# Two groups of heads share one burst of value sums, one copy, one turn and one normalisation in a two-layer gated cross-attention kernel

## The chip, the core and the metric

One core of a Trainium2 chip. The metric is the device time of one execution in microseconds (us). The engines are TensorE (PE, with its weight loads as PEld), VectorE (DVE), ScalarE (ACT), GpSimd (POOL) and SyncE (SP), which issues nearly all DMAs.

## What is computed

32 images of 256 tokens with 256 channels pass through two layers. The change lies in the first one, attention over the 120 context rows and the 256 tokens of the image itself, 16 heads of 16 channels:

```python
def _L0_xattn_ref(x, context, w_qkv, w_proj, b_proj):      # x here is layernorm(x)
    qkv = (x @ w_qkv.T).reshape(B, N, 3, H, D).transpose(2, 0, 3, 1, 4)
    q, k, v = (qkv[0], qkv[1], qkv[2])
    kv = context.reshape(B, N_c, 2, H, D).transpose(2, 0, 3, 1, 4)
    k = jnp.concatenate([kv[0], k], axis=2)
    v = jnp.concatenate([kv[1], v], axis=2)
    attn = jax.nn.softmax(jnp.einsum('bhnd,bhmd->bhnm', q * scale, k), axis=-1)
    out = jnp.einsum('bhnm,bhmd->bhnd', attn, v)
    return out.transpose(0, 2, 1, 3).reshape(B, N, C) @ w_proj.T + b_proj
x = x + tanh(g_xattn[0]) * _L0_xattn_ref(layernorm(x), ctx_2048, ...)
```

A ternary linear layer, a gated recurrence with a linear layer and an int8 linear layer follow. They run in a second phase of the kernel ("rows") that the change doesn't touch.

## The kernel before

**Phases.** All images stay in SBUF (`xs`). The attention phase (`*_attention`) goes over the images in `iterations`, from -3 to 32, since an image is prepared up to three iterations ahead and finished in the one after its own. Then the rows phase does the other three layers.

**An iteration** has 24 slots (`HS`, variable `u`). In slot u TensorE makes the transposed scores of two heads for one tile of 128 keys: two matmuls into one of three banks `st_ps` (L682, `scores_t`). ScalarE turns them into probabilities by one exp of 128x512 (L1022) into a ring of 12 tiles (`PR`), `probs`. A slot's scores need the exp of three slots before. Three k-tiles times two pairs, six slots, make up one group of four heads (`HG`), and there are four groups (`NG`).

**Maxima.** The exps need the row maxima of the scores, which go into the transposed product as three more rows of the queries. So TensorE also makes each head's scores the other way round (`scores`, L692, 376 keys wide, two banks `ms_ps`), 32 of them in an iteration, one or two a slot (`maxima_of`), mostly for the next image. VectorE reduces each to negated maxima (L932). POOL splits the maxima into three bf16 parts (`split_neg`, L535 to L541), TensorE turns them (jobs `neg0` and `neg1`, L748, weights of 24 columns), ScalarE copies them (`neg_rows`, L1029), and SP moves them by DMA into the queries' rows (L449, L466). neg1 is for the second half of the image's slots (12 on), neg0 for the first half of the next image.

**Value sums.** When a group's six slots are through, `attend` multiplies its three k-tiles with the values: per k-tile four heads side by side, each a product with weights of 32 columns (16 values, a one for the sum of the probabilities, and zeros) into 32 partitions of `pv_ps`. The matmuls are f32 and stand as two each in the trace, 24 for the 12 of a group (L707). The bursts stand in slots 7, 13, 19 and, for the last group, in slot 1 of the next iteration. ScalarE copies `pv_ps` to `oT` (`copy_o`, L1035, slots 8, 14, 20 and 2), TensorE turns it in two transposes (jobs `o0` to `o3`, L754, slots 10, 16, 22 and 4) into the bank `aux`, and VectorE takes the reciprocal of the sums (L939) and multiplies (L941, `normalise`), which frees the bank. At last `aT` (L759) turns the four groups' `attn`, ScalarE copies it, and `proj` multiplies with the output weights (L738); VectorE adds the result to `xs` (`update`, L974).

**What sets the order.** Two tables written out by hand. `JOBS` gives every TensorE job its bank (0 is `misc`, 1 is `aux`), its first slot, its number of slots and the image that it is for. A job waits until the job before it in its bank is taken, whoever takes it: q, k, v and xT by ScalarE, proj by VectorE's update; in `aux` kcT, neg and aT by ScalarE, o by VectorE. `AT` gives ScalarE's and VectorE's small steps their slots: ScalarE does a slot's small steps and then its exp, VectorE a slot's first maximum, the small steps and the slot's further maxima. All five engines run their queues in order. In a slot TensorE does the transposed scores, one row of maxima scores, the jobs in the table's order, a burst if there is one, and the rest of the maxima's scores.

**Queries and keys.** Jobs xT (L722), q and k (L730) and v (L733) make them from the normalised image; ScalarE copies q (L1070), k (L1090) and the context's keys `kc` (L1059) into `qk`. POOL splits `qk` into three bf16 parts (L552 to L558), half by half, with `split_neg` for neg0 between the halves. SP's ten DMAs a half (`stack`, L432 to L437) bring the parts into place, and SP issues the DMA of neg0 (L466) between the two halves.

Of the kernel before, what the change touches and what calls it, by code (L numbers as in the profile page):

```python
# [15 lines left out]
def flamingo_two_layers(  # L16
# [38 lines left out]
    NG = H // HG  # L55
    HS = NG * NKT * 2
# [28 lines left out]
    with ExitStack() as ctx:  # L85
# [51 lines left out]
        oT = sb("oT", [P, S])  # L137
        rcp = sb("rcp", [P, T, 4])
# [184 lines left out]
        def live(b):  # L323
# [9 lines left out]
        }  # L333
        AT = {
            "cxp": 0, "xnT": 1, "copy_o": 2, "kc": 4, "csq": 5, "q": 6, "aT": 5, "neg1": 7, "xn": 13, "k": 11, "decay": 17,
            "vcx": 14, "neg0": 19, "v": 23,
            "stats0": 0, "aggr0": 5, "norm": 4, "update": 19, "stats1": 20, "aggr1": 23, "mx": 6, "mn": 7,
# [287 lines left out]
        def tensor_attention(pe):  # L625
# [44 lines left out]
            def body(i, par):  # L670
# [24 lines left out]
                def attend(B, pB, w):  # L695
# [3 lines left out]
                    if k == 0:  # L699
                        wait(pe, s_oT, B * NG + g)  # L700
# [5 lines left out]
                    for j in range(HG):  # L706
                        mm = pe.matmul(pv_ps[VW * j:VW * (j + 1), 0:S], v[0:rows, pB, k, HG * g + j, :],  # L707
                                       probs[0:rows, (2 * w + j // 2) % PR, j % 2 * S:(j % 2 + 1) * S],
                                       start=(k == 0), stop=(k == NKT - 1), skip_group_check=True)
                    mm.then_inc(s_pv, 1)  # L710

                def make(name, part, off):
# [37 lines left out]
                    elif name[0] == "o":  # L750
                        g = int(name[1])
                        pe.wait_ge(s_oT, (b + off) * NG + g + 1)
                        for t in range(T):
                            mm = pe.transpose(aux[:, t * P:(t + 1) * P], oT[:, t * P:(t + 1) * P], ident[:, :])  # L754
                    elif name == "aT":
                        wait_taken(pe, b, "o3")
# [14 lines left out]
                for u in range(HS):  # L771
# [30 lines left out]
        def vector_attention(dve):  # L802
# [121 lines left out]
            def body(i, par):  # L924
# [539 lines left out]
```

## Time and profile before

| | us |
|---|---|
| Median of three runs | 1093.32 (1092.88 to 1097.19) |
| The profiled execution | 1093.88, its span 1092.1 |
| TensorE busy | 1029.8 (94%) |
| VectorE busy | 875.0 (80%) |
| ScalarE busy | 794.0 (73%) |
| GpSimd busy | 699.0 (64%) |

The attention phase takes the first 900 us of the span and the rows phase the rest. TensorE's granted clock is full in the attention phase. A busy time is the union of an engine's instructions; the ends of matmuls are modelled, and matmuls overlap each other in the array, so for TensorE the distance from one start to the next tells more than the durations. In a timeline like instructions in a row are merged into one line, with the first one's start and their count.

### The profile page before, as it was taken

What the parts mean: (1) busy time and instruction counts of PE and PEld (TensorE: products, weight loads), DVE (VectorE), ACT (ScalarE), POOL (GpSimd) and SP (SyncE); (2) the same over time, 40 slices, a digit from 0 to 9 for tenths busy, and PEclk for the clock granted to TensorE, in tenths of its full rate; (3) what the DMA queues carried; (4) which work ended last, traced back from release to release, by engine and by line L of the source; (5) the groups of instructions that cost most, each with busy time, mean ns of one, the idle gap of its engine ahead of it and who ended that gap; (6) DMA issues with size and microseconds to landing.
All of it is one profiled execution on the core that took longest, in us unless ns stands there. A gap on an engine that the chain in (4) does not pass through costs nothing. (4 is left out here: it accounts for less than half of the span.)

```text
span 1092.1 us, 26149 instructions
## 1 busy us (share of the span) xinstructions
PE 1029.8 (94%) x8522; PEld 706.0 (65%) x8522; DVE 875.0 (80%) x2218; ACT 794.0 (73%) x1731; POOL 699.0 (64%) x1348
## 2 busy tenths in 40 slices
PE   4799999999999999999999999999999967999994
PEld 3356666666666666666666666666666545888873
DVE  6767888878888878888887888888778765999996
ACT  3367777777777777777777777777777647999983
POOL 6556666666666666666666666666665214677776
PEclk8799999999999999999999999999999987999997
DMA  7775555655555556555556555555555210233232
GB/s 147 102 114 110 116 108 107 106 105 106 113 114 108 106 106 110 111 111 108 115 113 111 109 109 108 109 112 111 100 101 92 57 33 25 69 105 102 96 112 78
DMA packets 140906, 111.29 MB, mean 102 GB/s; under 512 B 15650, under 2 KB 136932, under 8 KB 140772
## 3 DMA queue, kind: packets, MB, share of 16 engines
q1 hardware_dynamic: 140068, 109.07, 49.6%
q8 instruction: 69, 1.13, 0.5%
q10 hardware_dynamic: 704, 0.55, 0.3%
q14 instruction: 65, 0.53, 0.2%
HBM read 30.33 MB, written 16.32 MB: 43 GB/s over the span
## 5 line engine op out<-in xcount | busy, mean ns | idle before, releaser
L932 DVE TENSOR_REDUCE neg<-ms_ps 128x1 f32<-128x376 f32 x1024 | 526.5, 544 | 160.1 <-PE ms_ps L692 154.3
L1022 ACT ACTIVATE probs<-st_ps 128x512 f32<-128x512 f32 x768 | 442.5, 603 | 25.2 <-PE st_ps L682 24.6
L692 PE MATMUL ms_ps<-qk 96*128 96x376 bf16 x1024 | 334.4, 327 | 11.6 <-DMA qk<-parts 5.7
L682 PE MATMUL st_ps<-qk 99*128 99x256 bf16 x1536 | 294.9, 274 | 0.7 <-DMA qk<-negT 0.7
L682 PEld LDWEIGHTS st_ps<-qk 99*128 99x128 bf16 x1536 | 133.7, 98 | 125.8 <-issue 41.4
L707 PE MATMUL pv_ps<-probs,v 128*32 128x256 f32 (+1 forms) x3072 | 194.4, 383 | 0.0
L730 PE MATMUL misc<-xnT,wqkvT 128*128 128x256 f32 x512 | 154.9, 386 | 1.7 <-DVE wqkvT L814 0.9
L692 PEld LDWEIGHTS ms_ps<-qk 96*128 96x128 bf16 x1024 | 98.8, 97 | 76.6 <-DVE neg L932 49.6
L707 PEld LDWEIGHTS pv_ps<-probs,v 128*32 128x32 f32 (+1 forms) x3072 | 96.1, 110 | 55.8 <-ACT probs L1022 12.3
L552 POOL TENSOR_SCALAR parts<-qk 128x632 bf16<-128x632 f32 x63 | 45.7, 725 | 125.1 <-ACT qk L1090 125.1
L730 PEld LDWEIGHTS misc<-xnT,wqkvT 128*128 128x128 f32 x512 | 92.1, 194 | 6.5 <-ACT qk L1070 1.8
L1029 ACT COPY negT<-aux 24x256 bf16<-24x256 bf16 x64 | 22.9, 357 | 97.3 <-PE aux L748 97.3
L558 POOL TENSOR_TENSOR parts<-qk,parts 128x632 bf16<-128x632 f32 x63 | 88.1, 1398 | 5.2
L554 POOL TENSOR_TENSOR qk<-qk,parts 128x632 f32<-128x632 f32 x63 | 87.8, 1394 | 5.2
L535 POOL TENSOR_SCALAR negp<-neg 128x16 bf16<-128x16 f32 x64 | 13.1, 205 | 103.2 <-DVE neg L932 103.2
L738 PE MATMUL misc<-wprojT,attnT 128*128 128x256 f32 x256 | 77.3, 385 | 0.8 <-ACT attnT L1073 0.8
L1244 PE MATMUL st_ps<-winT,probs 128*128 128x256 f32 x256 | 70.0, 396 | 8.2 <-ACT probs L1378 8.1
L733 PE MATMUL misc<-wqkvT,xnT 128*128 128x256 f32 x256 | 77.2, 382 | 0.0
L1244 PEld LDWEIGHTS st_ps<-winT,probs 128*128 128x128 f32 x256 | 46.3, 191 | 19.2 <-ACT probs L1378 13.8
L1035 ACT COPY oT<-pv_ps 128x256 f32<-128x256 f32 x128 | 47.5, 371 | 4.4 <-PE pv_ps L707 4.2
L754 PE MATMUL aux<-ident,oT 128*128 128x128 f32 x256 | 48.8, 272 | 0.6 <-ACT oT L1035 0.6
L1090 ACT COPY qk<-misc 128x512 f32<-128x512 f32 x32 | 18.8, 587 | 41.9 <-PE misc L730 41.9
(201 smaller groups left out, 1757.0 us busy)
## 6 DMA issues: line engine op xcount, KB each, us to landing
qk<-parts SPq DMA_DIRECT2D x253, 94.0 KB, 3.6
qk<-parts SPq DMA_DIRECT2D x128, 158.0 KB, 3.6
qk<-parts SPq DMA_DIRECT2D x256, 64.0 KB, 3.5
out_dram<-xn SPq DMA_DIRECT2D x32, 256.0 KB, 2.2
xs<-in_x SPq DMA_DIRECT2D x31, 256.0 KB, 2.9
cx<-in_ctx SPq DMA_DIRECT2D x32, 240.0 KB, 4.0
recurrence_input<-u_in SPq DMA_DIRECT2D x32, 120.0 KB, 2.8
plug<-plugs SPq DMA_DIRECT2D x32, 120.0 KB, 3.4
```

Source lines behind the costliest of these rows:

```text
L554: pool.tensor_tensor(f, f, parts[:, m, 0, :], ALU.subtract).then_inc(s_split, 1)
L558: pool.tensor_tensor(parts[:, m, 2, :], f, parts[:, m, 1, :], ALU.subtract).then_inc(s_split, 1)
L682: mm = pe.matmul(st_ps[u % SR][:, j * S:(j + 1) * S], k6[0:KM, r, h, k * P:(k + 1) * P], q6[0:KM, r, h, :], start=True, stop=True)
L692: pe.matmul(ms_ps[t][:, 0:KEYS], q6[0:KR, r, h % HU, t * P:(t + 1) * P], k6[0:KR, r, h % HU, 0:KEYS], start=True, stop=True).then_inc(s_ms, 1)
L707: mm = pe.matmul(pv_ps[VW * j:VW * (j + 1), 0:S], v[0:rows, pB, k, HG * g + j, :], probs[0:rows, (2 * w + j // 2) % PR, j % 2 * S:(j % 2 + ...
L730: mm = pe.matmul(misc[:, x0 * S:(x0 + 1) * S], wqkvT[:, x1, at:at + P], xnT[:, par, x1, :], start=(x1 == 0), stop=(x1 == KT - 1), skip_gro ...
L733: mm = pe.matmul(misc[:, x0 * C:(x0 + 1) * C], xnT[:, opp, x1, x0 * P:(x0 + 1) * P], wqkvT[:, x1, 2 * C:3 * C], start=(x1 == 0), stop=(x1 ...
L738: mm = pe.matmul(misc[:, x0 * C:(x0 + 1) * C], attnT[:, x1, x0 * P:(x0 + 1) * P], wprojT[:, x1, :], start=(x1 == 0), stop=(x1 == KT - 1), ...
L754: mm = pe.transpose(aux[:, t * P:(t + 1) * P], oT[:, t * P:(t + 1) * P], ident[:, :])
L932: dve.tensor_reduce(neg[:, m, t, h % HU:h % HU + 1], ms_ps[t][:, 0:KEYS], AX.X, ALU.max, negate=True).then_inc(s_red, 1)
L1022: act.activation(probs[:, u % PR, :], st_ps[u % SR][:, :], ACT.Exp).then_inc(s_exp, 1)
L1244: pe.matmul(m1_ps[q][:, t * C:(t + 1) * C], yxT[:, k, t * P:(t + 1) * P], winT[:, k, :], start=(k == 0), stop=False)
```

## The change

`pv_ps` has 512 columns, of which 256 were used. Now groups 0 and 1 go into its two halves in one burst of six k-tiles in slot 13, and groups 2 and 3 in one in slot 1 of the next iteration. One copy of 128x512, four transposes, one reciprocal and one multiplication take the place of two each. The jobs o0 to o3 become o0 and o1. In both tables other steps get new slots: the maxima's turns neg1 (slot 7 to 6) and neg0 (20 to 19), kcT (2 to 3), and on ScalarE and VectorE cxp, xnT, copy_o, q, aT, xn, k, decay, vcx, neg0, aggr0, update, stats1, mx and mn.

```diff
+    NH = NG // 2
-        oT = sb("oT", [P, S])
-        rcp = sb("rcp", [P, T, 4])
+        oT = sb("oT", [P, 2, S])
+        rcp = sb("rcp", [P, T, 2 * HG])
         JOBS = {
             "xT": (0, 1, 1, 2), "q": (0, 3, 4, 2), "k": (0, 8, 4, 2), "proj": (0, 15, 4, -1), "v": (0, 20, 4, 1),
-            "kcT": (1, 2, 1, 2), "o3": (1, 4, 1, -1), "aT": (1, 5, 1, -1), "neg1": (1, 7, 1, 0), "o0": (1, 10, 1, 0),
-            "o1": (1, 16, 1, 0), "neg0": (1, 20, 1, 1), "o2": (1, 22, 1, 0),
+            "kcT": (1, 3, 1, 2), "o1": (1, 4, 1, -1), "aT": (1, 5, 1, -1), "neg1": (1, 6, 1, 0), "o0": (1, 16, 1, 0),
+            "neg0": (1, 19, 1, 1),
         }
         AT = {
-            "cxp": 0, "xnT": 1, "copy_o": 2, "kc": 4, "csq": 5, "q": 6, "aT": 5, "neg1": 7, "xn": 13, "k": 11, "decay": 17,
-            "vcx": 14, "neg0": 19, "v": 23,
-            "stats0": 0, "aggr0": 5, "norm": 4, "update": 19, "stats1": 20, "aggr1": 23, "mx": 6, "mn": 7,
+            "cxp": 1, "xnT": 0, "copy_o": 4, "kc": 4, "csq": 5, "q": 7, "aT": 6, "neg1": 7, "xn": 12, "k": 12, "decay": 21,
+            "vcx": 11, "neg0": 20, "v": 23,
+            "stats0": 0, "aggr0": 0, "norm": 4, "update": 18, "stats1": 23, "aggr1": 23, "mx": 1, "mn": 6,
         }
...
-                    if k == 0:
-                        wait(pe, s_oT, B * NG + g)
+                    if k == 0 and g % 2 == 0:
+                        wait(pe, s_oT, B * NH + g // 2)
-                        mm = pe.matmul(pv_ps[VW * j:VW * (j + 1), 0:S], v[0:rows, pB, k, HG * g + j, :],
+                        mm = pe.matmul(pv_ps[VW * j:VW * (j + 1), g % 2 * S:(g % 2 + 1) * S], v[0:rows, pB, k, HG * g + j, :],
...
-                        g = int(name[1])
-                        pe.wait_ge(s_oT, (b + off) * NG + g + 1)
+                        half_ = int(name[1])
+                        pe.wait_ge(s_oT, (b + off) * NH + half_ + 1)
                         for t in range(T):
-                            mm = pe.transpose(aux[:, t * P:(t + 1) * P], oT[:, t * P:(t + 1) * P], ident[:, :])
+                            for g in range(2):
+                                mm = pe.transpose(aux[:, t * S + g * P:t * S + (g + 1) * P], oT[:, g, t * P:(t + 1) * P], ident[:, :])
...
                     if u == 1 and live(b - 1):
-                        for k in range(NKT):
-                            attend(b - 1, opp, (NG - 1) * NKT + k)
-                    elif u % (2 * NKT) == 1 and u > 1 and live(b):
-                        for k in range(NKT):
-                            attend(b, par, (u // (2 * NKT) - 1) * NKT + k)
+                        for w in range(NH * NKT, NG * NKT):
+                            attend(b - 1, opp, w)
+                    elif u == HS // 2 + 1 and live(b):
+                        for w in range(NH * NKT):
+                            attend(b, par, w)
...
-                def normalise(B, g):
+                def normalise(B, half_):
-                    wait_full(dve, b, f"o{g}")
-                    o4 = aux[:, 0:T * P].rearrange("p (t j c) -> p t j c", t=T, c=VW)
+                    wait_full(dve, b, f"o{half_}")
+                    o4 = aux[:, :].rearrange("p (t j c) -> p t j c", t=T, c=VW)
...
                     if u == AT["norm"] and live(b - 1):
-                        normalise(b - 1, 3)
-                    if u > AT["norm"] and u % 6 == AT["norm"] % 6 and live(b):
-                        normalise(b, (u - AT["norm"]) // 6 - 1)
+                        normalise(b - 1, 1)
+                    if u == AT["norm"] + HS // 2 and live(b):
+                        normalise(b, 0)
...
-                def copy_o(B, g):
-                    act.wait_ge(s_pv, (B * NG + g + 1) * NKT)
-                    if not (isinstance(b, int) and B * NG + g == 0):
-                        wait_full(act, b - (g == 3), f"o{(g - 1) % NG}")
-                    act.copy(oT[:, :], pv_ps[:, 0:S]).then_inc(s_oT, 1)
+                def copy_o(B, half_):
+                    act.wait_ge(s_pv, (B * NH + half_ + 1) * 2 * NKT)
+                    if B * NH + half_ > 0:
+                        wait_full(act, b - half_, f"o{1 - half_}")
+                    act.copy(oT[:, :, :], pv_ps[:, :].rearrange("p (g r) -> p g r", g=2)).then_inc(s_oT, 1)
```

ScalarE's calls of `copy_o` change like VectorE's of `normalise`.

## Rows read from the trace of the kernel before

**Rows 1.** The page, busy us, share of the span and instructions.

```profile
PE 1029.8 (94%) x8522; PEld 706.0 (65%) x8522; DVE 875.0 (80%) x2218; ACT 794.0 (73%) x1731; POOL 699.0 (64%) x1348
```

**Rows 2.** Line L974 between 400 and 700: duration in ns, first and last start.

```profile
L974 DVE SCALAR_TENSOR_TENSOR xs<-misc,tg,xs x11: 741/743/744, 414.7 to 678.0; 128x512 f32<-128x512 f32 x11
```

**Rows 3.** TensorE's timeline: start us, us from first start to last end, instructions.

```profile
521.23 0.59 PE L733 MATMUL misc<-wqkvT,xnT 128*128 128x256 f32 x2
521.76 0.28 PE L748 MATMUL aux<-identb,negp 128*24 128x128 bf16 x2
521.97 0.39 PE L682 MATMUL st_ps<-qk 99*128 99x256 bf16 x2
...
525.90 0.60 PE L722 MATMUL misc<-ident,xn 128*128 128x128 f32 x4
526.43 1.50 PE L707 MATMUL pv_ps<-probs,v 128*32 128x256 f32 x24
527.87 0.39 PE L682 MATMUL st_ps<-qk 99*128 99x256 bf16 x2
...
533.18 0.23 PE L748 MATMUL aux<-identb,negp 128*24 128x128 bf16 x1
...
534.69 0.39 PE L682 MATMUL st_ps<-qk 99*128 99x256 bf16 x2
...
541.16 0.32 PE L692 MATMUL ms_ps<-qk 96*128 96x376 bf16 x1
541.32 0.38 PE L682 MATMUL st_ps<-qk 99*128 99x256 bf16 x2
541.54 0.32 PE L692 MATMUL ms_ps<-qk 96*128 96x376 bf16 x1
541.70 0.60 PE L738 MATMUL misc<-wprojT,attnT 128*128 128x256 f32 x2
542.14 0.32 PE L692 MATMUL ms_ps<-qk 96*128 96x376 bf16 x1
542.30 0.38 PE L682 MATMUL st_ps<-qk 99*128 99x256 bf16 x2
542.58 0.33 PE L692 MATMUL ms_ps<-qk 96*128 96x376 bf16 x1
...
551.38 0.39 PE L682 MATMUL st_ps<-qk 99*128 99x256 bf16 x2
```

**Rows 4.** Waits between 400 and 700: us in total, times, longest.

```profile
DVE neg L932 <- PE ms_ps L692: 52.1, 81, 1.4
...
PEld ms_ps L692 <- DVE neg L932: 13.1, 72, 0.2
```

**Rows 5.** Groups between 400 and 700: busy us, mean ns, idle before.

```profile
L932 DVE TENSOR_REDUCE neg<-ms_ps 128x1 f32<-128x376 f32 x365 | 187.9, 544 | 54.0 <-PE ms_ps L692 52.1
...
L941 DVE TENSOR_TENSOR attn<-aux,rcp 128x128 f32<-128x128 f32 x45 | 13.1, 291 | 1.5
...
L1090 ACT COPY qk<-misc 128x512 f32<-128x512 f32 x12 | 7.0, 587 | 14.3 <-PE misc L730 14.3
```

**Rows 6.** ScalarE's timeline, exps and the copy of k.

```profile
523.09 1.55 ACT L1022 ACTIVATE probs<-st_ps 128x512 f32<-128x512 f32 x3
...
538.70 0.59 ACT L1090 COPY qk<-misc 128x512 f32<-128x512 f32 x1 [1.19 <-PE misc L730]
```

**Rows 7.** VectorE's timeline, maxima and the reciprocal.

```profile
541.52 1.99 DVE L932 TENSOR_REDUCE neg<-ms_ps 128x1 f32<-128x376 f32 x4 [1.37 <-PE ms_ps L692]
543.61 0.21 DVE L939 RECIPROCAL rcp<-aux 128x8 f32<-128x8 f32 x1
```

**Rows 8.** GpSimd's timeline, the last part of neg0.

```profile
546.23 0.22 POOL L541 TENSOR_TENSOR negp<-neg,negp 128x16 bf16<-128x16 f32 x1
```

**Rows 9.** SyncE's timeline, the DMA of neg0.

```profile
548.79 0.77 SPq L466 DMA_DIRECT2D qk<-negT  x1
```

**Rows 10.** ScalarE's timeline, the last copy of the attention phase.

```profile
888.10 0.37 ACT L1035 COPY oT<-pv_ps 128x256 f32<-128x256 f32 x1 [0.76 <-PE pv_ps L707]
```

More of the change, by code:

```diff
@@ L750, in make @@
                     elif name[0] == "o":
-                        g = int(name[1])
-                        pe.wait_ge(s_oT, (b + off) * NG + g + 1)
+                        half_ = int(name[1])
+                        pe.wait_ge(s_oT, (b + off) * NH + half_ + 1)
                         for t in range(T):
-                            mm = pe.transpose(aux[:, t * P:(t + 1) * P], oT[:, t * P:(t + 1) * P], ident[:, :])
+                            for g in range(2):
+                                mm = pe.transpose(aux[:, t * S + g * P:t * S + (g + 1) * P], oT[:, g, t * P:(t + 1) * P], ident[:, :])
                     elif name == "aT":
-                        wait_taken(pe, b, "o3")
+                        wait_taken(pe, b, "o1")
                         for t in range(T):
@@ L933, in maximum @@
                                       negate=True).then_inc(s_red, 1)
-                def normalise(B, g):
-                    wait_full(dve, b, f"o{g}")
-                    o4 = aux[:, 0:T * P].rearrange("p (t j c) -> p t j c", t=T, c=VW)
+                def normalise(B, half_):
+                    wait_full(dve, b, f"o{half_}")
+                    o4 = aux[:, :].rearrange("p (t j c) -> p t j c", t=T, c=VW)
                     dve.reciprocal(rcp[:, :, :], o4[:, :, :, D]).then_inc(s_rcp, 1)
-                    dve.wait_ge(s_rcp, B * NG + g + 1)
-                    dve.tensor_tensor(attn[:, :, g * HG * D:(g + 1) * HG * D].rearrange("p t (j d) -> p t j d", d=D),
-                                      o4[:, :, :, 0:D], rcp[:, :, :].unsqueeze(3).broadcast_to([P, T, HG, D]),
+                    dve.wait_ge(s_rcp, B * NH + half_ + 1)
+                    dve.tensor_tensor(attn[:, :, half_ * P:(half_ + 1) * P].rearrange("p t (j d) -> p t j d", d=D),
+                                      o4[:, :, :, 0:D], rcp[:, :, :].unsqueeze(3).broadcast_to([P, T, 2 * HG, D]),
                                       ALU.mult).then_inc(s_free[1], 1)
@@ L1049, in body @@
                     if u == AT["copy_o"] and live(b - 1):
-                        copy_o(b - 1, 3)
-                    if u > AT["copy_o"] and u % 6 == AT["copy_o"] % 6 and live(b):
-                        copy_o(b, (u - AT["copy_o"]) // 6 - 1)
+                        copy_o(b - 1, 1)
+                    if u == AT["copy_o"] + HS // 2 and live(b):
+                        copy_o(b, 0)
                     if u == AT["kc"] and live(b + 2):
```

## The prediction

> **What bounds the kernel now.** The page's busy times come first: TensorE is at 94%, VectorE at 80%, ScalarE at 73% [rows 1]. That is no proof of a bound, because the ends of matmuls are modelled. The row of the residual update comes next: in the steady stretch it starts 11 times between 414.7 and 678.0, so one image takes 263.3 / 10 = 26.33 us [rows 2]. TensorE's timeline then shows how far one instruction starts behind the one before it (its pitch). A pair of transposed score matmuls has 0.22 (541.32 to 541.54), a score matmul over all keys 0.16 (541.54 to 541.70), a pair of f32 matmuls 0.43 (541.70 to 542.14), and so a f32 transpose of 128 columns, half the columns of one matmul of such a pair, 0.11; the stream follows itself at these pitches nearly everywhere [rows 3]. Weight loads waited 13.1 us of 300 for VectorE, and that is their longest wait for any engine [rows 4]. So the sum of the pitches on TensorE sets the period, and the others matter where TensorE reaches an instruction whose operand or bank isn't there.
>
> Of the image from 527.87 to 554.19 I add what stands above the pitches for no structural reason: 542.30 to 542.58 is 0.28 for 0.22, and with six more such places of 0.02 to 0.07 it comes to 0.35 us [rows 3]. The rest, 26.33 - 0.35 = 25.98, is pure stream.
>
> The Trainium skill would judge otherwise: its page Perfetto Trace Analysis, section Identifying the Most-Contended Engine, takes TensorE by the busy share of weight loads, here 65% [rows 1], and calls the engine with the highest occupancy the one to look at, here VectorE. By it the time would be that of rival 3.
>
> **What the change does to TensorE's stream.** No matmul goes away: 96 for the values and 8 transposes an image stay. The four bursts of three products become two of six. One burst costs more than its columns. Six rounds at the f32 pitch of 0.215 are 1.30; the burst takes 526.43 to 527.87, 1.44. Ahead of it four transposes that start at 525.90 are through at 526.34, and the burst starts 0.09 later [rows 3]. Together 0.23 us, so two bursts fewer give **-0.46**. That a burst of 12 rounds keeps the 0.215 isn't in the trace; bounds are 0.215 (six rounds) and 0.24 (1.44 / 6), at the upper one the whole gain is gone, and I take the lower since nothing in a burst has to be reloaded in another way at the seam.
>
> The maxima's transpose neg1 moves from slot 7, where the burst follows it at once, to slot 6, where no burst is. Beside a burst it adds 1.51 - 1.44 = 0.07 (533.18 to 534.69). Alone it costs what neg0 costs alone: 0.09 ahead of it (the f32 pair at 521.23 is through at 521.66) and 0.21 to the next instruction, 0.30 [rows 3]. **+0.23**.
>
> Both have weights of 32 columns or fewer, everything around them 128. The Trainium skill, TensorEngine Tiling (Array Packing), section Key Properties, says that a change of the tiling mode drains the engine; by this rule the move of neg1 makes a new pair of switches, as the 0.09 at either side shows.
>
> Stream: 25.98 - 0.46 + 0.23 = 25.75 us.
>
> **What the other engines do.** ScalarE: four copies of 256 columns at 0.37 [rows 10] become two of 512, 0.59 each as the copy of the keys [rows 5]: 1.48 to 1.18. VectorE: reciprocal 0.21 [rows 7] and product 0.29 [rows 5], four times, 2.00. The product of 256 elements isn't in the trace: its bounds are 0.29 and 0.54 (376 elements, L932) [rows 5]; on the line between them, 1.0 ns an element, it is 0.42. 2 x (0.22 + 0.42) = 1.28. Neither saving is on the path; both hide behind TensorE. They count only through when things come free, so I walk through the slots. Starts are in us from the first score matmul after a burst; exp follows exp at 0.49 (three in 1.55) [rows 6], an instruction starts 0.04 after the matmul it waits for (541.16 + 0.32, and VectorE at 541.52), a score pair ends 0.39 after its start, TensorE goes on 0.05 after a release by VectorE (a maximum that began at 541.52 + 0.48 is done at 542.53, the matmul is at 542.58) and by my estimate up to 0.11 where f32 weights must be loaded first [rows 3, 7].
>
> First half (slots 2 to 13):
> - o1, slot 4: it needs copy_o and kc, both in ScalarE's slot 4. exp 2 at 0.43, exp 3 at 0.91, copy_o 1.40, kc 1.89 to 2.31, released 2.42; TensorE is there at 2.40 (three score pairs 0.67, four maxima rows 0.65, two f32 pairs of q 0.87, kcT 0.21). +0.03.
> - aT, slot 5, needs the product. The last of the four transposes starts at 2.75, the reciprocal 0.31 later (543.30 to 543.61 today), the product 0.24 after it, to 3.72: released 3.83, TensorE there 3.83. 0.
> - neg1, slot 6, needs the bank that ScalarE's copy aT frees in the same slot: 4.47 to 5.06. TensorE is there at 5.17 (3.83, aT 0.44, pair 0.22, row 0.16, q 0.43, the 0.09). 0, with 0.06 to spare.
> - k, slot 8, needs q copied (slot 7 now, behind exp 6): released 6.16 (exp 6 at 4.96, q 5.44 to 6.05); TensorE is there at 6.15 (5.17, neg1 0.21, two pairs and two rows 0.77). +0.02.
> - a maximum late at slot 11: VectorE's chain of maxima at 0.48 [rows 7]: +0.07.
> - exp 12 takes the ring's slot of exp 0 and so must wait for the burst's first product, some 0.3 us. TensorE asks for exp 12 only at slot 15: 0.
>
> Second half: maximum at slot 16 +0.06 (542.30 to 542.58 has it today [rows 3]); o0 at slot 16: copy_o out at 2.09, TensorE there 2.25, 0; the longer product holds the next maximum to 4.00, TensorE wants its bank at 3.88 (2.25, o0 0.44, two rows, two pairs, proj 0.43): **+0.18** at slot 18; v behind the update, +0.04; slot 23, +0.06; xT behind the copy of v, +0.14, where today the DMA of negT stops TensorE just before (0.05). Sum of both halves: 0.12 + 0.48 = 0.60.
>
> Past the queues: k's copy moves to slot 12 behind xn on ScalarE, which is what POOL waits for. By the walk it ends 10.8 us in, against 11.42 today (538.70 + 0.59 - 527.87 [rows 3, 6]). POOL's chain from there to the rows of neg0 takes 7.16 (to 546.23 + 0.22 [rows 8]), so 17.95; TensorE gets to neg0, now slot 19, at 18.1: hidden by 0.15 only. SP: the DMA of negT starts at 19.2 and the score that needs it can start 2.6 later (548.79 to 551.38 [rows 3, 9]), 21.8 against 22.1: hidden. vcx at 11, decay at 21, statistics at 0 and 23, mx at 1 and cxp at 1 lie under bursts or in idle time (ScalarE idles 1.19 us before k alone [rows 6]): 0.
>
> **Sum.** 25.75 + 0.60 = 26.35 against 26.33: **+0.02** an image, +0.6 over the 29 at this period. The last burst is six products, not three: by its 1.3, and copy, transposes and product by 0.2, 0.2 and 0.1, the last image ends later (today ScalarE waits 0.76 us for the burst before the copy at 888.10 [rows 10]), +1.8; image 0 has a burst of three less, -1.3, and its k copy comes behind xn, +0.5. In all about +1.7. The profiled execution took 1093.88 (span 1092.1), 0.56 over the median; 1093.3 + 1.7 = **1095.0 us**.
>
> **Rivals.** About 0.5% (5.5 us) is what a measurement of this kernel tells from no change; that is 0.19 us an image.
> 1. *Waits vanish.* The releases come as early as today and the product isn't on the way: only 0.35 or less stays above the stream. For: VectorE has 0.7 and ScalarE 0.3 less to do. Against: the slot numbers leave gaps of 0.1 where there were two slots. 25.75 + 0.25 to 0.35 gives -0.23 to -0.33 an image, 1085 to 1088.
> 2. *The closer slots bind (the other side).* The aux bank passes TensorE, ScalarE, TensorE within a slot at 4, 6 and 16, and v follows the update. One mechanism: a release that comes 0.1 to 0.15 later than walked, at five places, stops the stream each time. +0.35 an image, 1105; past 0.15 an image it is slower than the bound. For: the gaps are 0 to 0.15. Against: the constants repeat to 0.01 from image to image, as the 26.33 does.
> 3. *VectorE is the bound*: a maximum's release sets each maximum's row, and what VectorE saves all comes off, 0.72 an image, 21 us, 1074. For: its 80% [rows 1]. Against: it idles 52.1 of 300 us while it waits for TensorE [rows 4].
> 4. *It doesn't do what it says*: it takes no work from TensorE at all; that it then changes nothing is in the forecast.
>
> **Chances.** Forecast (1089 to 1100) 0.50; rival 1 0.27; rival 2 0.20; rival 3 0.03. Faster by over 0.5% is rivals 1 and 3 less 0.02 that ends just within, 0.28; slower is rival 2 and 0.02 of the forecast's upper edge, 0.22; within, 0.50. For 8 in 10 the range takes rival 1 and the nearer part of rival 2: 1084 to 1103.
>
> **What would show it.** Update to update 26.2 to 26.5 (rival 1 under 26.1, rival 2 over 26.5); bursts of 48 in 2.73; neg1 alone with 0.30 around it; copy_o 0.59; the product 0.42; the maximum at slot 18 late by 0.2; VectorE's idle time up, TensorE's stops 0.6 an image. A period that changes while these stops don't would make the walk wrong; a score matmul of slot 0 or neg0 that waits for DMA or POOL would mean that a chain that I call hidden isn't.

## The result, and the profile after

The changed kernel is slower by 2%, outside the predicted range.

| | before | after |
|---|---|---|
| Median of the runs on one chip, us | 1093.71 (1092.88 to 1097.19), 4 runs | 1116.53 (1115.71 to 1117.45), 4 runs |
| Ratio to before | | 1.0198 (95%: 1.0182 to 1.0215) |
| The profiled execution, us | 1093.88, span 1092.1 | 1115.71, span 1113.9 |

The page of the changed kernel, for [rows 1], and below it one of the groups of the whole run (busy us, mean ns, idle before and what ended it), with the same group of the kernel before as the last line:

```profile
PE 1033.1 (93%) x8522; PEld 699.6 (63%) x8522; DVE 860.6 (77%) x2090; ACT 809.2 (73%) x1667; POOL 700.4 (63%) x1348
...
L683 PE MATMUL st_ps<-qk 99*128 99x256 bf16 x1536 | 294.8, 273 | 16.8 <-DMA qk<-negT 15.4
...
L682 PE MATMUL st_ps<-qk 99*128 99x256 bf16 x1536 | 294.9, 274 | 0.7 <-DMA qk<-negT 0.7
```

VectorE has 128 instructions less, four an image as the merge says, and 14.4 us less of busy time; TensorE still has its 8522 matmuls. No share tells of a loss. The group does: score matmuls now wait 15.4 us for the DMA of the turned maxima, where they waited 0.7.

The residual update between 400 and 700, for [rows 2]:

```profile
L976 DVE SCALAR_TENSOR_TENSOR xs<-misc,tg,xs x11: 741/743/744, 423.1 to 692.8; 128x512 f32<-128x512 f32 x11
```

269.7 / 10 = 26.97 us an image, against 26.33. Over 29 images in the middle, from one copy of the keys to the next, the trace gives 27.00 against 26.34: +0.66 x 29 = +19.2 of the 21.8 us that the span grew. Up to the first of these copies the changed kernel takes 1.3 less (one burst less stands ahead of it), and from the last copy of the keys to the end it takes 3.9 more.

Waits between 400 and 700, for [rows 4]; the last line is one of the kernel before that [rows 4] leave out:

```profile
DVE neg L934 <- PE ms_ps L693: 58.4, 80, 2.6
...
PEld ms_ps L693 <- DVE neg L934: 17.3, 77, 0.4
...
PEld st_ps L683 <- DMA qk<-negT: 10.3, 12, 1.2
DVE rcp L941 <- PE aux L756: 6.2, 22, 0.3
PE st_ps L683 <- DMA qk<-negT: 5.6, 10, 0.8
...
PEld st_ps L682 <- DMA qk<-negT: 2.0, 7, 0.4
```

VectorE waits longer for TensorE than before (58.4 for 52.1), so it isn't the bound. The wait of a score matmul for this DMA was there before, at the weight loads alone: 2.0 us in seven images. Now it is 10.3 us at the weight loads and another 5.6 us, in ten of eleven images, at the matmuls.

TensorE's timeline, for [rows 3]. The first lines are the part behind slot 1, the last ones the seam between two images:

```profile
515.95 0.60 PE L731 MATMUL misc<-xnT,wqkvT 128*128 128x256 f32 x2
516.47 0.63 PE L761 MATMUL aux<-ident,attn 128*128 128x128 f32 x4
...
517.32 0.60 PE L731 MATMUL misc<-xnT,wqkvT 128*128 128x256 f32 x2
517.84 0.28 PE L749 MATMUL aux<-identb,negp 128*24 128x128 bf16 x2
518.06 0.39 PE L683 MATMUL st_ps<-qk 99*128 99x256 bf16 x2
...
523.00 2.81 PE L708 MATMUL pv_ps<-probs,v 128*32 128x256 f32 x48
525.74 0.39 PE L683 MATMUL st_ps<-qk 99*128 99x256 bf16 x2
...
534.44 0.60 PE L734 MATMUL misc<-wqkvT,xnT 128*128 128x256 f32 x2
535.49 0.39 PE L683 MATMUL st_ps<-qk 99*128 99x256 bf16 x2 [0.46 <-DMA qk<-negT]
```

- The burst of 48 takes 523.00 to 525.74, 2.74; two bursts of 24 took 2.88. With the 0.09 that each has ahead of it, two bursts fewer are 0.46 an image, as forecast.
- neg1 by itself (517.32 to 518.06) is 0.43 of the pair ahead of it, 0.09, and 0.21 to the next instruction: the forecast 0.30.
- The last pair of `v` starts at 534.44 and would be followed 0.43 later by the score matmul of slot 0. This starts at 535.49: a **stop of 0.62**, where the image of [rows 3] had one of 0.05.

The other stops above the pitches, in this image: aT 0.11 (walked as 0; 0.09 of it is the start at 516.47, 0.52 behind a pair of 0.43), k 0.04 (0.02), slot 11 0.06 (0.07), slot 16 0.06 (0.06), slot 18 0.23 (0.18), v 0.05 (0.04), slot 23 0.06 (0.06), xT 0 (0.14; the DMA's stop just ahead of it covers it). Together 1.24, and 26.95 - 1.24 = 25.71 of stream, against 25.75 in the forecast.

SyncE's timeline at that seam:

```profile
524.51 0.59 SPq L433 DMA_DIRECT2D qk<-parts  x1
...
527.76 0.53 SPq L472 DMA_DIRECT2D cx<-in_ctx  x1
...
530.86 0.61 SPq L436 DMA_DIRECT2D qk<-parts  x1
531.75 0.76 SPq L467 DMA_DIRECT2D qk<-negT  x1
```

and ScalarE's, with the copy of the keys that starts this chain and the copy of neg0's turn:

```profile
522.91 0.56 ACT L1092 COPY qk<-misc 128x512 f32<-128x512 f32 x1
...
531.38 0.35 ACT L1031 COPY negT<-aux 24x256 bf16<-24x256 bf16 x1
```

The DMA of neg0 is issued at 531.75 and the score starts at 535.49, 3.74 later; before it was 2.59 [rows 3, 9]. From the end of the keys' copy (523.47) the issue is 8.28 behind, before 9.50. So neg0 came **earlier** in the chain, as forecast, and its data came later than forecast. What was issued ahead of it has its sizes in the page's list of transfers (KB each, us from issue to landing):

```profile
qk<-parts SPq DMA_DIRECT2D x253, 94.0 KB, 3.6
qk<-parts SPq DMA_DIRECT2D x128, 158.0 KB, 3.7
qk<-parts SPq DMA_DIRECT2D x256, 64.0 KB, 3.5
```

Ten of them go out ahead of neg0's 12 KB between 524.51 and 530.86 (two of 158, four of 94, four of 64: 948 KB), and the context's 240 KB in their midst. The engines in windows of 1 us (window: us, then each engine's busy time and instructions, the granted clock of TensorE, the DMA engines' share, GB/s):

```profile
530.00:531.00 1.00, 1.00 (x8) 0.58 (x7) 1.00 (x3) 0.54 (x2) 0.83 (x4) 1.00 1.03 222
531.00:532.00 1.00, 1.00 (x8) 0.65 (x8) 1.00 (x3) 1.00 (x3) 0.92 (x2) 1.00 1.22 144
532.00:533.00 1.00, 1.00 (x7) 0.74 (x6) 0.74 (x2) 1.00 (x3) 0.91 (x2) 1.00 1.09 121
533.00:534.00 1.00, 1.00 (x9) 0.60 (x7) 0.95 (x3) 0.62 (x2) 0.92 (x2) 1.00 1.24 134
534.00:535.00 1.00, 1.00 (x6) 0.45 (x4) 1.00 (x3) 0.02 (x1) 1.00 (x1) 1.00 0.62 98
```

On average all sixteen DMA engines are taken up (a share of 1.0 and more) from before the issue until 534, and the score starts 1.5 us behind that.

**How the chain sets the period.** I read the end of the keys' copy, the slot-0 score and the next keys' copy in all 29 middle images of each trace (us; the columns "chain" and "rest" add up to the period). The landing is the last update that the trace has of this DMA's semaphore, again behind the keys' copy:

| kernel | chain: keys' copy to slot-0 score, least, mean, most | landing of neg0's DMA, least, median, most | rest: score to the next keys' copy, typical | period, mean |
|---|---|---|---|---|
| before | 11.93, 12.09, 12.41 | 11.66, 11.91, 12.37 | 14.29 | 26.34 |
| after | 11.40, 12.08, 12.51 | 11.29, 12.06, 12.46 | 14.93 | 27.00 |

After, the rest is 14.93 or 14.94 in 27 of 29 images while single periods go from 26.4 to 27.4: nearly the whole scatter lies in the chain. Its least value, 11.40, is TensorE's own stream (the walk said 22.1 - 10.8 = 11.3); in the other 28 images the score starts 0.05 behind the landing. Before, that stream needed 12.04 (but in the first of the 29), and the data came at nearly the same 11.91: in 17 images it was in time. In the other 12, that of [rows 3] among them, the score waited for it by 0.02 to 0.44 us.

### The profile page after: what moved, and what is told of

It reads as the page before. It is cut to its first block and busy times, and to the rows that moved or that the text cites. A ratio compares the mean times of both kernels' runs of the same rounds, so it can differ in the third digit from the quotient of the medians.

```text
span 1113.9 us, 25766 instructions
## 1 busy us (share of the span) xinstructions
PE 1033.1 (93%) x8522; PEld 699.6 (63%) x8522; DVE 860.6 (77%) x2090; ACT 809.2 (73%) x1667; POOL 700.4 (63%) x1348
## 5 line engine op out<-in xcount | busy, mean ns | idle before, releaser
L934 DVE TENSOR_REDUCE neg<-ms_ps 128x1 f32<-128x376 f32 x1024 | 518.0, 544 | 181.1 <-PE ms_ps L693 176.3
L683 PE MATMUL st_ps<-qk 99*128 99x256 bf16 x1536 | 294.8, 273 | 16.8 <-DMA qk<-negT 15.4
L683 PEld LDWEIGHTS st_ps<-qk 99*128 99x128 bf16 x1536 | 137.4, 98 | 122.4 <-DMA qk<-negT 27.2
L708 PE MATMUL pv_ps<-probs,v 128*32 128x256 f32 (+1 forms) x3072 | 179.5, 381 | 0.0
L708 PEld LDWEIGHTS pv_ps<-probs,v 128*32 128x32 f32 (+1 forms) x3072 | 93.3, 109 | 69.2 <-issue 13.3
L553 POOL TENSOR_SCALAR parts<-qk 128x632 bf16<-128x632 f32 x63 | 45.7, 726 | 108.3 <-ACT qk L1092 108.3
L557 POOL TENSOR_SCALAR parts<-qk 128x632 bf16<-128x632 f32 x63 | 45.5, 722 | 5.5
L600 POOL TENSOR_TENSOR xs<-xs,bias_p 128x256 f32<-128x256 f32 x64 | 45.7, 735 | 5.0 <-DVE ginit L821 5.0
L734 PEld LDWEIGHTS misc<-wqkvT,xnT 128*128 128x128 f32 x256 | 44.5, 194 | 4.3 <-issue 0.2
L739 PEld LDWEIGHTS misc<-wprojT,attnT 128*128 128x128 f32 x256 | 45.5, 193 | 2.0 <-issue 1.0
```

The costliest lines, as they stand in the source:

```text
L553: pool.tensor_scalar(parts[:, m, 0, :], f, 1.0, 0.0, ALU.mult, ALU.add).then_inc(s_split, 1)
L683: mm = pe.matmul(st_ps[u % SR][:, j * S:(j + 1) * S], k6[0:KM, r, h, k * P:(k + 1) * P], q6[0:KM, r, h, :], start=True, stop=True)
L708: mm = pe.matmul(pv_ps[VW * j:VW * (j + 1), g % 2 * S:(g % 2 + 1) * S], v[0:rows, pB, k, HG * g + j, :], probs[0:rows, (2 * w + j // 2) % ...
L734: mm = pe.matmul(misc[:, x0 * C:(x0 + 1) * C], xnT[:, opp, x1, x0 * P:(x0 + 1) * P], wqkvT[:, x1, 2 * C:3 * C], start=(x1 == 0), stop=(x1 ...
L739: mm = pe.matmul(misc[:, x0 * C:(x0 + 1) * C], attnT[:, x1, x0 * P:(x0 + 1) * P], wprojT[:, x1, :], start=(x1 == 0), stop=(x1 == KT - 1), ...
L934: dve.tensor_reduce(neg[:, m, t, h % HU:h % HU + 1], ms_ps[t][:, 0:KEYS], AX.X, ALU.max, negate=True).then_inc(s_red, 1)
```

## The experiments

Each kernel of the table was run beside the kernel before; the medians of that kernel's runs were 1094.35 (e1 to e4), 1094.57 (e5 to e8) and 1094.58 (e9).

| kernel | us | ratio, 95% | period from the update's row |
|---|---|---|---|
| e1 | 1101.87 | 1.0068 (1.0050 to 1.0087) | 26.45 |
| e2 | 1101.97 | 1.0071 (1.0050 to 1.0093) | 26.54 |
| e3 | 1116.47, one run | | 26.98 |
| e4 | 1137.52 | 1.0398 (1.0372 to 1.0424) | 27.71 |
| e5 | 1101.70, one run | | 26.59 |
| e6 | 1087.08 | 0.9928 (0.9912 to 0.9945) | 26.09 |
| e7 | 1090.21 | 0.9957 (0.9941 to 0.9974) | 26.17 |
| e8 | 1114.64, one run | | 26.91 |
| e9 | 1112.52 | 1.0177 (1.0158 to 1.0197) | 26.89 |

The questions: is the stop at slot 0 made by what stands ahead of neg0's DMA, or does that transfer simply take 3.7 us here, or is the loss in the new slots of other steps?

### e1: neg0's DMA ahead of the last two of the ten

```diff
                 for part, steps in ((0, 1), (1, 3), (2, 4)):
+                    if part == 2 and ahead:
+                        ahead()
...
-                    stack(b + 2, par, 0, load_cx if live(b + 3) and live(b) else None)
-                if live(b + 1) and live(b):
+                    stack(b + 2, par, 0, load_cx if live(b + 3) and live(b) else None,
+                          rows_0 if live(b) else None)
+                elif live(b + 1) and live(b):
                     rows_0()
```

> The changed kernel, with one edit: SyncE issues the DMA of neg0's rows ahead of the last two of the ten DMAs of queries and keys instead of behind all ten. Theory A (the rows' DMA is served in order behind the transfers of the ten, which start with k's copy): it starts at the same time or a little earlier, has less in front of it and lands some 2.6 us after its issue, not 3.7. The first score matmul of an image then waits under 0.15 us instead of 0.62, an image takes 26.4 to 26.5 us instead of 26.97, the kernel some 15 us less, 1099 to 1103. Rival B (a DMA at this place takes 3.7 us whatever stands before it, only the time of ScalarE's copy counts): no change, 26.97 and 1116. Rival C (the loss comes from ScalarE and VectorE, which stand still under the longer burst, and the first score would wait for something else at once): 26.8 or more.

Measured: 1101.87, 14.7 us less than the changed kernel, and 26.45 an image. The update's row, SyncE's and TensorE's timelines:

```profile
L979 DVE SCALAR_TENSOR_TENSOR xs<-misc,tg,xs x11: 740/741/743, 416.9 to 681.4; 128x512 f32<-128x512 f32 x11
```

```profile
497.25 0.77 SPq L469 DMA_DIRECT2D qk<-negT  x1
498.07 0.58 SPq L440 DMA_DIRECT2D qk<-parts  x1
...
500.38 0.38 PE L686 MATMUL st_ps<-qk 99*128 99x256 bf16 x2
```

The keys' copy ends at 488.98, so neg0 is issued at the same 8.28 as in the changed kernel, but the score follows at 11.40, without a wait, in 26 of 29 images (the others up to 11.59). The one edit takes away the stop and nearly all scatter. Of the 0.66 that the period had grown, 0.09 stay (26.43 against 26.34, mean of 29). The stop of xT comes back with 0.13, as walked. The landing is now 10.89 behind the keys' copy (median; 12.06 in the changed kernel). This is the same computation, the same slots and the same bytes: the order of eleven DMAs on one queue is worth 14.7 us.

### e2: the keys' job copied one slot earlier

```diff
-            "cxp": 1, "xnT": 0, "copy_o": 4, "kc": 4, "csq": 5, "q": 7, "aT": 6, "neg1": 7, "xn": 12, "k": 12, "decay": 21,
+            "cxp": 1, "xnT": 0, "copy_o": 4, "kc": 4, "csq": 5, "q": 7, "aT": 6, "neg1": 7, "xn": 12, "k": 11, "decay": 21,
```

> The changed kernel with k's copy on ScalarE back in slot 11, ahead of xn; nothing else. The DMA of neg0's rows is issued when it was. Theory A: k's copy ends some 0.6 us earlier, the ten DMAs start and end so much earlier, and the first score, 12.03 us after k's copy in the changed kernel, comes 0.5 to 0.6 earlier: an image takes 26.4 to 26.5, the kernel 1099 to 1103. Rival B: nothing of k's copy reaches the first score, 26.97 and 1116, or slower since ScalarE waits for k ahead of exp 11. Rival C: 26.8 or more.

Measured: 1101.97. The copy, then neg0's DMA behind all ten again:

```profile
489.73 0.58 ACT L1092 COPY qk<-misc 128x512 f32<-128x512 f32 x1 [1.05 <-PE misc L731]
...
499.13 0.77 SPq L467 DMA_DIRECT2D qk<-negT  x1
```

The queue's order is as in the changed kernel. TensorE's stream from the copy to the score is now 11.94 instead of 11.40, and the landing is at 11.96 (median), as before. The chain is 11.94 to 12.41 in 27 of 29 images (in the other two 12.94 and 14.15): small stops are left in about half the images. So the slot of one ScalarE copy and the order on SyncE's queue are two cures of one thing, and each takes away nearly the same 14.6 us.

### e3: neg0 turned one slot later

```diff
-            "neg0": (1, 19, 1, 1),
+            "neg0": (1, 20, 1, 1),
```

> The changed kernel with TensorE's turn of neg0 in slot 20 instead of 19, so that ScalarE's copy and the rows' DMA come 0.7 to 0.9 us later; nothing else. Theory A: the first score still starts some 12.0 us after k's copy, as the DMA arrives in the queue while the ten are still being served; an image takes 26.95 to 27.15. Rival B: the score follows 3.7 us after the later issue, an image takes 27.7 or more and the kernel some 20 us more than the changed one.

Measured: one run, 1116.47. The DMA and the score:

```profile
506.62 0.76 SPq L467 DMA_DIRECT2D qk<-negT  x1
...
509.13 0.39 PE L683 MATMUL st_ps<-qk 99*128 99x256 bf16 x2
```

The issue is 1.08 later (9.36 behind the keys' copy in place of 8.28) and the score is not: the chain is 12.04 in the mean against 12.08, here 2.51 from issue to score instead of 3.74. A transfer that takes 3.7 us by itself is ruled out: when it is asked for later, it comes at the same time (landing 12.04, median). The edit has a second effect: neg0 no longer stands ahead of `v` and gives the update time, so v's stop in slot 20 is 0.36. It lengthens TensorE's own stream to 11.71, still under the landing, and so the period stays.

### e4 and e8: the merge in the old slots

e4 is the changed kernel with every other step in its old slot (the last copy's in slot 2, turned in slot 4, the first one's in 14 and 16).

```diff
-            "kcT": (1, 3, 1, 2), "o1": (1, 4, 1, -1), "aT": (1, 5, 1, -1), "neg1": (1, 6, 1, 0), "o0": (1, 16, 1, 0),
-            "neg0": (1, 19, 1, 1),
+            "kcT": (1, 2, 1, 2), "o1": (1, 4, 1, -1), "aT": (1, 5, 1, -1), "neg1": (1, 7, 1, 0), "o0": (1, 16, 1, 0),
+            "neg0": (1, 20, 1, 1),
         }
         AT = {
-            "cxp": 1, "xnT": 0, "copy_o": 4, "kc": 4, "csq": 5, "q": 7, "aT": 6, "neg1": 7, "xn": 12, "k": 12, "decay": 21,
-            "vcx": 11, "neg0": 20, "v": 23,
-            "stats0": 0, "aggr0": 0, "norm": 4, "update": 18, "stats1": 23, "aggr1": 23, "mx": 1, "mn": 6,
+            "cxp": 0, "xnT": 1, "copy_o": 2, "kc": 4, "csq": 5, "q": 6, "aT": 5, "neg1": 7, "xn": 13, "k": 11, "decay": 17,
+            "vcx": 14, "neg0": 19, "v": 23,
+            "stats0": 0, "aggr0": 5, "norm": 4, "update": 19, "stats1": 20, "aggr1": 23, "mx": 6, "mn": 7,
```

> The merged bursts, copies, turns and normalisations of the change, but every other step in the slots that it had before (neg1 at 7, neg0 at 20, k's copy at 11, xn at 13 and so on; copy_o at 2 and 14, o1 at 4, o0 at 16). By my own steps TensorE's stream is 25.75 us an image, k's copy ends near 10.4 us after the burst and the first score can start near 22.4, where TensorE arrives at about 22.2. Theory A: stops of 0.4 to 0.6, 26.1 to 26.4 an image, 1087 to 1095: the merge alone doesn't slow the kernel, the new slots do. Rival C (the merged burst itself costs what was lost): 26.8 or more, over 1108.

A miss: 1137.52, slower than both. It took the slots to be free of the bursts, and they are not. `v` starts in slot 20 in the bank that the update (slot 19) has to free. Before, a burst stood in slot 19 and gave the update its time; now none does. TensorE and VectorE at that place:

```profile
513.65 0.32 PE L693 MATMUL ms_ps<-qk 96*128 96x376 bf16 x1
...
514.10 0.74 DVE L976 SCALAR_TENSOR_TENSOR xs<-misc,tg,xs 128x512 f32<-128x512 f32 x1
...
514.89 0.70 PE L734 MATMUL misc<-wqkvT,xnT 128*128 128x256 f32 x2 [0.92 <-DVE xs L976]
```

From 513.65 to 514.89 is 1.24 for the 0.16 of a maxima row: a stop of 1.08. e8 moves the update alone back to slot 18.

```diff
-            "stats0": 0, "aggr0": 5, "norm": 4, "update": 19, "stats1": 20, "aggr1": 23, "mx": 6, "mn": 7,
+            "stats0": 0, "aggr0": 5, "norm": 4, "update": 18, "stats1": 20, "aggr1": 23, "mx": 6, "mn": 7,
```

> The merged bursts with all other steps in their old slots (27.70 us an image), with one edit: the residual update on VectorE in slot 18 instead of 19. There v's first matmul stood 1.08 us for the bank that the update frees, since no burst lies between them any more. In slot 18 the update starts some 0.9 us earlier: the stop falls to 0.1 to 0.3, an image takes 26.7 to 26.95. If v waits for another thing, 27.7 stays.

Measured: one run, 1114.64, and 26.91 an image; v's stop is 0.36 in place of 1.18 (the row above with 0.10 behind it). So 0.8 of the period goes with that stop, and the move of the update to 18, which the prediction didn't price, was needed by the merge. What is left above the pitches in an image of e8 is v 0.36, slot 18 0.23, xT 0.13, aT 0.11, a maxima row behind the first two of k's pairs 0.10, and 0.22 in five small places, together 1.15; on the stream of 25.75 that makes the 26.9 without any rest. The DMA isn't in it: it is issued 9.89 behind the keys' copy and lands at 12.11 (medians), ahead of TensorE's 12.25. Issued that late it takes 2.21.

### e5: neg1's slot alone, in the kernel before

```diff
-            "kcT": (1, 2, 1, 2), "o3": (1, 4, 1, -1), "aT": (1, 5, 1, -1), "neg1": (1, 7, 1, 0), "o0": (1, 10, 1, 0),
+            "kcT": (1, 2, 1, 2), "o3": (1, 4, 1, -1), "aT": (1, 5, 1, -1), "neg1": (1, 6, 1, 0), "o0": (1, 10, 1, 0),
```

> The kernel before with one edit: TensorE's turn neg1 in slot 6 instead of slot 7, away from the burst, everything else as before. By the step of the prediction that costs the move at 0.23 us an image, TensorE's stream gets 26.33 + 0.23 = 26.56 (26.5 to 26.6), 6 to 7 us for the kernel. If the turn costs the same beside a burst and alone (the rival reading of the two rows), 26.33 stays.

Measured: one run, 1101.70. TensorE's timeline:

```profile
511.15 0.59 PE L730 MATMUL misc<-xnT,wqkvT 128*128 128x256 f32 x2
511.68 0.28 PE L748 MATMUL aux<-identb,negp 128*24 128x128 bf16 x2
511.89 0.39 PE L682 MATMUL st_ps<-qk 99*128 99x256 bf16 x2
```

The f32 pair has its 0.43, then 0.10, then 0.21. The mean of 29 periods goes from 26.34 to 26.58, +0.24: the price of a product with 24 columns of weights that is taken away from a burst. This term of the sum is shown by itself.

### e9: neg0's DMA on another queue

ScalarE issues it behind its own copy, on its own queue; SyncE's queue keeps the ten. The two calls of `rows_0` go too.

```diff
-                def rows_0():
-                    own_wait_taken(sp, b, "neg0")
-                    sp.dma_start(q6[KR:KM, 2 * opp, :, :], negT[:, 0, :]).then_inc(d_neg[2 * opp], 16)
...
                         neg_rows(b + 1, i + (par + 1) // 2, opp, 0)
+                        own_wait_taken(act, b, "neg0")
+                        act.dma_start(q6[KR:KM, 2 * opp, :, :], negT[:, 0, :]).then_inc(d_neg[2 * opp], 16)
```

> The changed kernel with one edit: ScalarE, not SyncE, issues the DMA of neg0's rows, directly behind its own copy and at nearly the same time (some 0.1 to 0.3 us later), so in another queue than the ten DMAs of queries and keys, whose order and times stay. Theory A1 (the rows' DMA waits for its turn in SyncE's queue): in a queue of its own it lands in 2 to 2.7 us, the first score's stop goes from 0.62 to 0 to 0.2, an image takes 26.4 to 26.6, the kernel 1099 to 1105. Theory A2 (the 16 DMA engines themselves are behind, and any DMA has to wait there): the stop stays at 0.4 or more, 26.8 to 27.1 and 1110 or more.

Measured: 1112.52, and the period 26.89. The DMA and the score:

```profile
529.83 0.75 ACTq L1097 DMA_DIRECT2D qk<-negT  x1
...
533.55 0.39 PE L676 MATMUL st_ps<-qk 99*128 99x256 bf16 x2 [0.43 <-DMA qk<-negT]
```

Still 3.72 from issue to score; the chain is 11.40 to 12.28 in 28 of 29 images (12.64 in the first), 12.02 in the mean. A queue of its own brings 0.07 an image (27.00 to 26.93, mean of 29) where the place in the order brings 0.57. So a place in the queue of the large ones isn't what holds the small transfer. The windows of e9 behind the issue (columns as above):

```profile
530.00:531.00 1.00, 1.00 (x8) 0.71 (x6) 0.74 (x2) 0.31 (x1) 0.91 (x2) 1.00 1.10 123
531.00:532.00 1.00, 1.00 (x8) 0.60 (x7) 0.95 (x3) 1.00 (x4) 0.92 (x2) 1.00 1.09 112
```

The last of the ten was issued at 528.95, and the engines are full for three us more. This fits a wait of the 12 KB at the DMA engines, which both queues use, for what had been issued before; no view shows that wait itself.

### e6 and e7: a version that beats both

e6 has e1's order, the keys' copy in slot 11, and the first half's turn and normalisation in slot 23 in place of 16, where they held up the maxima; `mx` and `mn` go to slot 13, under the burst. The cut shows only the turn and the normalisation.

```diff
-            "kcT": (1, 3, 1, 2), "o1": (1, 4, 1, -1), "aT": (1, 5, 1, -1), "neg1": (1, 6, 1, 0), "o0": (1, 16, 1, 0),
+            "kcT": (1, 3, 1, 2), "o1": (1, 4, 1, -1), "aT": (1, 5, 1, -1), "neg1": (1, 6, 1, 0), "o0": (1, 23, 1, 0),
...
-                    if u == AT["norm"] + HS // 2 and live(b):
+                    if u == HS - 1 and live(b):
                         normalise(b, 0)
```

> The rows of neg0 ahead of the last two DMAs and k's copy in slot 11 (each took the wait of the first score away), and further: o0's turn and its normalisation in slot 23 instead of 16, mx and mn both in slot 13 under the burst. By the walk through the slots the stop of 0.23 at slot 18, which the longer normalisation makes, goes, and so does the 0.13 of xT behind v's copy, since o0's four transposes now lie between the two: 26.45 - 0.36 = 26.1 (26.0 to 26.2) an image, the kernel 1089 to 1094. If the stop at slot 18 comes from the update or from the maxima themselves, it stays and an image takes 26.35 or more.

Measured: 1087.08, ratio 0.9928 to before. The update's row:

```profile
L979 DVE SCALAR_TENSOR_TENSOR xs<-misc,tg,xs x12: 741/743/743, 409.0 to 696.0; 128x512 f32<-128x512 f32 x12
```

26.09 an image, 0.24 under before; the stops of slot 18 (0.23), of xT (0.13) and of the DMA are gone, while aT 0.11 and 0.04 to 0.06 at five other places stay. The period is what was expected; the time is 2 us under the expected one, so the allowance in it for the start and the end was too large. The sum is the prediction's: -0.46 for the bursts, +0.23 for neg1 alone, and as much of stops as before (0.36 for 0.35). So the merge is worth its 0.46 when it doesn't bring on a new wait.

e7, on top of e6, tried to take aT's stop away too, with kcT out of the way in slot 9. Not in this cut: ScalarE's wait for POOL's split moves from kc to q.

```diff
-            "kcT": (1, 3, 1, 2), "o1": (1, 4, 1, -1), "aT": (1, 5, 1, -1), "neg1": (1, 6, 1, 0), "o0": (1, 23, 1, 0),
+            "kcT": (1, 9, 1, 2), "o1": (1, 4, 1, -1), "aT": (1, 5, 1, -1), "neg1": (1, 6, 1, 0), "o0": (1, 23, 1, 0),
...
-            "cxp": 1, "xnT": 0, "copy_o": 4, "kc": 4, "csq": 5, "q": 7, "aT": 6, "neg1": 7, "xn": 12, "k": 11, "decay": 21,
+            "cxp": 1, "xnT": 0, "copy_o": 3, "kc": 10, "csq": 5, "q": 7, "aT": 6, "neg1": 7, "xn": 12, "k": 11, "decay": 21,
```

> As the one with o0 in slot 23, and kcT turned in slot 9 and copied in slot 10 (with the wait for the split moved to q's copy), copy_o in slot 3. o1 then doesn't stand behind kc's copy, the normalisation ahead of aT starts some 0.2 us earlier, and aT's stop of 0.11 goes: 25.95 to 26.05 an image, the kernel 1086 to 1091, under the kernel before. If aT waits for VectorE's maxima rather than for o1, nothing changes against the one with o0 in slot 23.

Measured: 1090.21, within the expected time, but 26.17 an image where 25.95 to 26.05 was expected: a miss of the mechanism. VectorE and TensorE between o1 and aT:

```profile
499.41 0.60 PE L759 MATMUL aux<-ident,oT 128*128 128x128 f32 x4
...
500.05 0.26 DVE L944 RECIPROCAL rcp<-aux 128x16 f32<-128x16 f32 x1 [0.32 <-PE aux L759]
500.34 0.42 DVE L946 TENSOR_TENSOR attn<-aux,rcp 128x256 f32<-128x256 f32 x1
...
500.91 0.63 PE L764 MATMUL aux<-ident,attn 128*128 128x128 f32 x4
```

The last transpose of o1 starts at 499.74 (0.33 behind the first), and aT 1.17 after it. That is a loop: 0.31 to the reciprocal, 0.29 to the product, 0.42, and 0.15 until TensorE goes on. Its own work in between is 1.09, in e6 as in e7, because the same instructions stand between o1 and aT. Moving kcT shifts both ends; only more work between them would hide it, which no run tried. The 0.08 more than in e6 is a maximum that kcT no longer gives time to, in the slot of o1: its row follows the score pair by 0.29 (498.52 to 498.81) instead of 0.22.

## Why the prediction was wrong

**The step that failed** is "SP: the DMA of negT starts at 19.2 and the score that needs it can start 2.6 later (548.79 to 551.38 [rows 3, 9]), 21.8 against 22.1: hidden". The 19.2 is right (19.17 measured) and TensorE's 22.1 nearly so (22.29). The 2.6 is wrong: it was 3.74. In the image that it was read from, 2.55 of the 2.59 were indeed the transfer (TensorE stood 0.05 for it), but it was no constant: there the transfer had been issued 1.22 us later in the chain, when more of the ten were through. The landing stays where the ten put it (29 images each, us behind the keys' copy):

| kernel | issue, median | landing, median | issue to landing, median | TensorE's stream to the score | images in which the score waited |
|---|---|---|---|---|---|
| before | 9.50 | 11.91 | 2.43 | 12.04 | 12 |
| after | 8.28 | 12.06 | 3.75 | 11.40 | 28 |
| e2, ten earlier against the stream | 8.82 | 11.96 | 3.10 | 11.94 | 16 |
| e3, issue later | 9.36 | 12.04 | 2.69 | 11.71 | 26 |
| e9, another queue | 8.28 | 12.03 | 3.72 | 11.40 | 27 |
| e1, ahead of the last two | 8.28 | 10.89 | 2.61 | 11.40 | 2 |

With all ten ahead of it the DMA lands at 11.9 to 12.1, whether it is issued at 8.28 or at 9.50. This could have been read from the trace of before: the score came 12.09 behind the keys' copy and waited for the DMA, in seven images of the stretch. In the changed order TensorE needs 11.40, and 12.08 - 11.40 = 0.68 an image is missing. The forecast moved one end of the chain by its slot and took the other for a constant from the issue. The runs show: the order decides, an earlier start of the ten decides, a later issue doesn't, and another queue hardly does. Whether the bytes of the large transfers count or their number of packets, no run separates.

Of the +0.66 in the period this is 0.57, measured by e1: 0.68 less xT's stop, which comes back when the DMA's goes.

**The stream** was right: 25.71 against 25.75. The burst's rounds keep 0.215 at the seam (2.74), the merge takes away 0.46, neg1 alone costs 0.24 (e5) against 0.23. The Trainium skill's TensorEngine Tiling (Array Packing), Key Properties, says that a change of the tiling mode drains the engine; the trace agrees, with about 0.1 us ahead of the product in e5, though no run here shows the mode itself.

**The stops** were walked as 0.60 with xT's 0.14 in it. Without the DMA's they are 0.62 in the changed kernel, and 0.75 with the 0.13 for xT that e1 shows. Six places (k, 11, 16, 23, v, xT) are within 0.02, o1 is 0 for 0.03. Slot 18 is 0.23 for 0.18, and aT 0.11 for 0: there the walk gave 0.24 from the reciprocal to the product and 0.11 for the restart, and measured are 0.29 (a reciprocal of 16 elements takes 0.26, not 0.22) and 0.15. The copy, taken as 0.59 from that of the keys, and the product, interpolated to 0.42, came out exactly. ScalarE's and VectorE's groups between 400 and 700:

```profile
L1037 ACT COPY oT<-pv_ps 128x512 f32<-128x512 f32 x22 | 13.0, 592 | 0.0
L943 DVE TENSOR_TENSOR attn<-aux,rcp 128x256 f32<-128x256 f32 x22 | 9.3, 425 | 0.8
L941 DVE RECIPROCAL rcp<-aux 128x16 f32<-128x16 f32 x22 | 5.7, 258 | 6.2 <-PE aux L756 6.2
```

With the DMA out of the way the period is 26.43 (e1) against the walk's 26.35.

**The ends** were mis-sized: by the prediction's terms +1.0 (-1.3 and +0.5 at the start, +1.8 at the end; with the +0.6 of the middle these make 1.6, where the prediction took 1.7), measured +2.6. The keys' copy, from which I count, ends 10.89 behind slot 2's score instead of 11.42, which makes the start shorter and the end longer by 0.5; without that the start is -0.7 (forecast -0.8) and the end +3.4 (forecast +1.8). Of the 3.4, 2.0 come before the last update of the phase, and 1.3 behind it, in the rows phase, whose code the change doesn't touch. There the granted clock differs: right behind the last update it is at the lower level (1.2 GHz) for 17.1 us before and for 20.5 us after. It sorts the runs: in the kernel before, e2, e5 and e9 it is 17.1 us there, and the kernel ends 197.2 to 197.6 us behind its last update; in the changed kernel, e3, e4, e6, e7 and e8 it is 20.5 us (in e1 27.3, from 4.5 ahead of the update on), and the end is 198.4 to 198.9 us behind. Since e2 and e9 have the merge too, this 1.3 isn't its price. (The clock isn't full throughout the attention phase either: in the first 60 us it is at the lower level for 20.5 us before and 23.9 us after.)

**The rivals.** The waits did not vanish: rival 1's sum assumed 0.35 of stops. VectorE as the bound (rival 3) is out, since it idles more and the period moved with a DMA. So the rule in the Trainium skill's Perfetto Trace Analysis, Identifying the Most-Contended Engine, read as in the prediction (weight loads 65%, VectorE 80%), would have misled here. By number rival 2 (1105) is nearest, but not by its mechanism: against the walk, releases came late by 0.05 and 0.11 at two places, not by 0.1 to 0.15 at five. The loss sits at one place that the rivals leave out and "What would show it" only names. No rival asked what stood ahead of neg0's DMA, though its 2.6 was the only transfer time in the sum.

**What stays open:** why the low clock behind the last update lasts 17.1 us in some runs and 20.5 in others; and why the chain takes 11.4 in some images and 12.5 in others (SyncE's issues are stretched in some of them, by up to 1.3 us, but they don't sort the images).

## What to carry to other kernels

A time from a DMA's issue to its landing holds only for what stood ahead of it at that issue (2.2 to 4.2 us here for the same 12 KB). Where an edit moves the issue against large transfers, take the whole chain from the work that sets these off, compare it with the stream of the engine at the far end, and ask which transfers stand ahead. A small transfer on which the next stage hangs goes ahead of large ones that have slack; moving it to another queue hardly helped here (0.07 of 0.66 us an image), while the DMA engines were full. A burst that goes away takes with it the cover of handshakes beside it, so after a merge every producer and consumer of a shared bank near the old place must be looked at again.

## What the runs showed of the hardware that I had not expected

- 12 KB on ScalarE's queue still took 3.72 us from issue to the waiting score, while SyncE's queue kept the sixteen engines at a share of 1.1 (e9); on the shared queue it was 3.74. Issued 1.08 later it took 2.51 (e3). To the landing, medians of 29 images: 3.72, 3.75 and 2.69; issued last of all, in e8, 2.21.
- TensorE restarts 0.15 after the product that releases a f32 transpose's operand (e7, 500.76 to 500.91), against 0.05 after a maximum (before, 542.53 to 542.58).
- A reciprocal of 128x16 takes 0.258 against 0.21 for 128x8: 6 ns for each element more, where the product's is 1.
